# TensorE adds the gathered rows of a graph layer, with chunks paired by kind, slots of 12 passes and edge records of 4

## The reference

```
msg = x[src] + edge_feat
agg = segment_sum(msg, dst, num_segments=12500)
h = relu(agg @ W1 + b1)            # 64 -> 128
out = layernorm(x + h @ W2 + b2)   # 128 -> 64
```

## Time and profile before

| | us |
|---|---|
| median of 3 runs | 1507.69 (1505.83 to 1508.44) |
| the profiled execution, its own time | 1504.08 |
| its span, first to last instruction | 1502.3 |

### The profile page before, as it was taken

How to read it: one execution, slowest core, us unless ns; L and a number is a source line. 1 busy time by engine, 2 the same in 40 slices (tenths; PEclk the granted TensorE clock), 3 DMA queues, 4 the chain that set the end, 5 groups by cost and what they waited for, 6 DMA issues and landing times.

```text
span 1502.3 us, 43214 instructions
## 1 busy us (share of the span) xinstructions
PE 1212.9 (81%) x15541; PEld 979.2 (65%) x15542; DVE 1346.7 (90%) x3537; ACT 840.6 (56%) x1767; POOL 1076.9 (72%) x1139
## 2 busy tenths in 40 slices
PE   1235767778787887888888888899999999999895
PEld 1134656655666776776655555688888888888853
DVE  4659999999999899899999999999999999999644
ACT  1044444668435566567444444567777777766454
POOL 9758777777777777777777777777777777777312
PEclk8555578999999999999999999999999999999997
DMA  2833444444444444444444443444444444433133
GB/s 103 212 85 79 120 113 111 116 111 109 108 115 112 114 115 106 108 109 116 112 114 107 104 117 102 113 112 111 112 112 109 111 113 113 113 100 94 23 79 93
DMA packets 159272, 162.50 MB, mean 108 GB/s; under 512 B 53817, under 2 KB 141801, under 8 KB 158729
## 3 DMA queue, kind: packets, MB, share of 16 engines
q1 hardware_dynamic: 124679, 122.86, 27.9%
q0 software_dynamic: 34384, 36.90, 12.8%
HBM read 154.78 MB, written 4.85 MB: 106 GB/s over the span
## 4 chain that ended last, share of the span: by engine, by line
PE 31%; DVE 29%; issue 16%; POOL 11%; DVEq 4%; ACT 2%; DMA 1%; POOLq 0%; ACTq 0%
PE sums_ps L1092 12%; PE counted_ps L1076 11%; POOL xmsg L572 11%; DVE oh_key L878 10%; DVE oh_lo L874 6%; PE chunk_ps L1059 5%; DVE onehot L835 5%; DVE lists L856 3%; DVE gmsg L828 2%; DVEq L848 2%; PE turn_ps L1104 2%; ACT counts L674 1%; DVE less_b L788 1%; DVEq L856 1%; PE counted_ps L1160 1%
## 5 line engine op out<-in xcount | busy, mean ns | idle before, releaser
L572 POOL DMA_INDIRECT xmsg<-in_x,idx_t x1025 | 995.5, 971 | 322.4 <-issue 307.8
L674 ACT CAST counts<-counted_ps 128x392 bf16<-128x392 f32 (+2 forms) x1375 | 675.2, 545 | 480.6 <-PE counted_ps L1076 468.1
L1076 PE MATMUL counted_ps<-oh_key,oh_lo 128*128 128x196 bf16 (+3 forms) x4206 | 524.7, 255 | 123.2 <-DVE oh_key L878 105.9
L878 DVE TENSOR_TENSOR oh_key<-counted_ps,tables 128x980 bf16<-128x980 f16 (+4 forms) x883 | 541.3, 613 | 0.0
L1092 PE MATMUL sums_ps<-x_parts,counts 128*128 128x193 bf16 (+4 forms) x4410 | 495.0, 249 | 0.3
L1076 PEld LDWEIGHTS counted_ps<-oh_key,oh_lo 128*128 128x128 bf16 x4206 | 290.5, 102 | 227.3 <-DVE oh_key L878 167.0
L1092 PEld LDWEIGHTS sums_ps<-x_parts,counts 128*128 128x128 bf16 (+4 forms) x4410 | 396.3, 109 | 38.6 <-issue 1.9
L874 DVE TENSOR_TENSOR oh_lo<-counted_ps,tables 128x640 bf16<-128x640 f16 (+3 forms) x883 | 412.3, 467 | 9.9 <-PE counted_ps L1076 1.0
L1059 PE MATMUL chunk_ps<-onehot,cmsg 128*64 128x32 f32 (+1 forms) x4200 | 254.1, 231 | 26.2 <-DVE gmsg L828 23.6
L1059 PEld LDWEIGHTS chunk_ps<-onehot,cmsg 128*64 128x64 f32 x4200 | 220.1, 145 | 60.9 <-issue 43.2
L835 DVE TENSOR_TENSOR onehot<-counted_ps,rel_t 128x160 f32<-128x160 f32 (+1 forms) x625 | 234.3, 375 | 0.2
(11 more groups left out here) (96 smaller groups left out, 450.2 us busy)
## 6 DMA issues: line engine op xcount, KB each, us to landing
cmsg<-in_edge_attr SPq DMA_DIRECT2D x420, 160.0 KB
gmsg<-in_edge_attr SPq DMA_DIRECT2D x205, 160.0 KB
xmsg<-in_x,idx_t POOLq DMA_INDIRECT x1025
x_parts<-in_x SPq DMA_DIRECT2D x12, 256.0 KB, 3.4
out_nodes<-x_parts SPq DMA_DIRECT2D x12, 256.0 KB, 2.6
edge_records<-counts SPq DMA_DIRECT2D x1, 1575.0 KB
lists<-in_src SPq DMA_DIRECT2D x1, 1562.5 KB
lists<-in_dst SPq DMA_DIRECT2D x1, 1562.5 KB
```

What stands on the lines that cost most here:

```text
L572: pool.indirect_dma_start(xmsg[:, at * D:(at + 1) * D], None, x, bass.IndirectOffsetOnAxis(ap=idx_t[:, of:of + 1], axis=0)).then_inc(gathe ...
L674: nc.scalar.copy(to, ps.rearrange("p (n h) -> p h n", h=HI)).then_inc(unit_kept, 1)
L878: nc.vector.tensor_tensor(oh_key[s % RING][:, 0:n * w].rearrange("p (k n o) -> p k n o", k=n, o=2), key_ps[:, 0:w].rearrange("p (n o) -> p ...
L1076: mm = nc.tensor.matmul(unit_ps[u % BANKS][:, col:col + slot.key_cols], oh_lo[s % RING][:, n * P:(n + 1) * P], oh_key[s % RING][:, n * slo ...
```

## The change

- `mix` is gone. For a gathered chunk TensorE multiplies the edge rows and then the gathered rows by the same mark, 10 matmuls a chunk instead of 5. `xmsg` has 6 slots instead of 5, freed by TensorE's products instead of by `mix`; `gmsg` has 6 instead of 8.
- Both chunks of a pair are of one kind, and one `mark` instruction makes the mark of both (313 instead of 625). `onehot` has 2 buffers of a pair instead of 4 of a chunk.
- Slots hold up to 12 nodes' worth of passes, and `plan` weighs widths by `85 + 86 * w` instead of `195 + 92 * w`.
- `FINE` is 4 instead of 16, so groups of edges begin at multiples of 4; a row of records is shorter, and 128 edges are still fetched at once. A pass of the search now has a stretch of its own (`Range`: first, step, length): row p of a group is loaded from `first + p * step`. An added small instruction (`begins`, from `row_at`) puts the row's offset to the result. Guard values stand at both ends of `fine_most`.
- `CROWS` is 86 instead of 84: 430 counted chunks and 195 gathered ones.
- Loads and stores with 125 or 86 rows are issued as two DMAs, one of them with a multiple of 16 rows (`in_sixteens`).
- The planned times in `timeline` change, and `TURN_TABLE` and `SUBTRACT` swap their slots.

By the arithmetic of `plan` and `timeline`, with N = 12500 and E = 400000:

| | before | after |
|---|---|---|
| counted nodes | 5716 | 5988 |
| passes of width 1, 2, 3, 4 | 1547, 2006, 75, 578 | 2666, 1545, 335, 0 |
| units of 5, 4, 3 nodes | 241, 1109, 25 | 411, 732, 335 |
| slots, groups, blocks | 883, 33, 45 | 581, 36, 48 |
| indirect gathers | 1025 | 975 |
| searched elements, all groups | 22842 | 29938 |
| slots of width 3 | 26 (of 3 or fewer passes) | 85, the last ones, nearly all of 4 passes and 4 units |

```diff
-            cost = sum(t * (195 + 92 * w) for t in ts) / nodes
+            cost = sum(t * (85 + 86 * w) for t in ts) / nodes
...
-        while (at + n < len(passes) and (at + n) % P and passes[at + n][2] == width and n < 10
-               and (n + 1) * width * hi <= 10 * hi):
+        while (at + n < len(passes) and (at + n) % P and passes[at + n][2] == width and n < SLOT
+               and (n + 1) * width <= SLOT):
...
+        for step in range(counted // FINE // P):
+            first = min(a - p * step for p, a in enumerate(low))
+            length = max(a - p * step for p, a in enumerate(high)) - first
+            if best is None or length < best.length:
+                best = Range(first, step, length)
...
-    cost = [x.n * (195 + 92 * x.width) + 500 for x in slots]
+    cost = [x.n * (67 + 51 * x.width) + 290 for x in slots]
...
-    FIRST, LAST = 90.0, 36.0 + 6.6 * gathered + 1.4 * groups
+    FIRST, LAST = 90.0, 36.0 + 6.45 * gathered + 1.4 * groups
...
+    pairs = [(36.0 + chunk * (k + 2) + 5.0, "gather", k) for k in range(0, gathered - 1, 2)]
+    pairs += [(70.0 + (LAST - 70.0) * (i + 1.) / counted, "count", i) for i in range(0, counted - 1, 2)]
+    pairs.sort()
...
-    GSLOTS, XSLOTS, CSLOTS = 8, 5, 6
+    GSLOTS, XSLOTS, CSLOTS = 6, 6, 6
...
+            for to, of, done in ((src_i, src_v, src_in), (dst_i, dst_v, dst_in)):
+                for a, b in in_sixteens(ROWS):
+                    sp.dma_start(to[a:b, :], of[a:b, :]).then_inc(done, 16)
...
+                sp.dma_start(most_b[g % 2][:, 0:x.length],
+                             bass.AP(most_dram.tensor, FRONT + x.first, [[x.step, P], [1, x.length]])).then_inc(most_in[g % 2], 16)
...
-                    pool.wait_ge(mixed, k - XSLOTS + 1)
+                    pool.wait_ge(summed, PLACE["gather", k - XSLOTS] + 1)
...
+                nc.vector.scalar_tensor_tensor(out=begins[g % 2][:, :], in0=row_at[:, :], scalar=float(x.step),
+                                               in1=run_t[:, g:g + 1], op0=ALU.mult, op1=ALU.add).then_inc(slanted, 1)
...
-            def mark(place, kind, i):
-                c = i if kind == "count" else CCH + i
-                if place >= OSLOTS:
-                    dve.wait_ge(summed, place - OSLOTS + 1)
-                w = width_of(kind, i)
+            def mark(pair):
+                (place, kind, i), n = pair[0], len(pair) * TILES
+                c, w = i if kind == "count" else CCH + i, width_of(kind, i)
+                if place >= 2 * OSLOTS:
+                    dve.wait_ge(summed, place - 2 * OSLOTS + 2)
...
-                pe.wait_ge(mixed, i + 1)
-                return gmsg[:, s * TILES * D:(s + 1) * TILES * D]
+                s, t = i % GSLOTS, i % XSLOTS
+                pe.wait_ge(gin[s], 16 * (i // GSLOTS + 1))
+                pe.wait_ge(gathered[t], 16 * TILES * (i // XSLOTS + 1))
+                return [gmsg[:, s * TILES * D:(s + 1) * TILES * D], xmsg[:, t * TILES * D:(t + 1) * TILES * D]]
```

More of the change, by code:

```diff
@@ L12 @@
 TOP = 256
-CROWS = 84
-FINE = 16
+CROWS = 86
+SLOT = 12
+FINE = 4
 RARE = 1e-7
@@ L19 @@
 Piece = namedtuple("Piece", "unit at cols opens closes")
+Range = namedtuple("Range", "first step length")
 def rare_above(mean, cap):
@@ L128, in timeline @@
         gathers_at[s].append(divmod(g, 5))
-    jobs = [(36.0 + chunk * (k + 1) + 5.0, "gather", k) for k in range(gathered)]
-    jobs += [(70.0 + (LAST - 70.0) * (i + .5) / counted, "count", i) for i in range(counted)]
-    jobs.sort()
+    pairs = [(36.0 + chunk * (k + 2) + 5.0, "gather", k) for k in range(0, gathered - 1, 2)]
+    pairs += [(70.0 + (LAST - 70.0) * (i + 1.) / counted, "count", i) for i in range(0, counted - 1, 2)]
+    pairs.sort()
     jobs_at = [[] for _ in range(S + 1)]
     s = 0
-    for place, (_, kind, i) in enumerate(jobs):
-        t = jobs[min(place | 1, len(jobs) - 1)][0]
+    for q, (t, kind, i) in enumerate(pairs):
         while s < S and begin[s] < t:
             s += 1
-        jobs_at[s].append((place, kind, i))
+        jobs_at[s] += [(2 * q, kind, i), (2 * q + 1, kind, i + 1)]
+    kind, i = ("gather", gathered - 1) if gathered % 2 else ("count", counted - 1)
+    jobs_at[S].append((2 * len(pairs), kind, i))
     return gathers_at, jobs_at
@@ L164, in build @@
     NARROW_ROWS = narrow_chunks(N, E, CHUNK, SLIM, CCH) // TILES
-    width_of = lambda kind, i: SLIM if kind == "count" and i < NARROW_ROWS * TILES else WIN
+    width_of = lambda kind, i: SLIM if kind == "count" and (i | 1) < NARROW_ROWS * TILES else WIN
     HI = -(-N // P)
@@ L265, in build @@
         xmsg = sb("xmsg", [P, XSLOTS * TILES * D])
[L266 to L268 removed]
+        onehot = [sb(f"onehot{s}", [P, 2 * TILES * WIN]) for s in range(OSLOTS)]
+        oh_lo = [sb(f"oh_lo{k}", [P, SLOT * P], bf16) for k in range(RING)]
+        oh_key = [sb(f"oh_key{k}", [P, SLOT * HI], bf16) for k in range(RING)]
         tables = [sb(f"tables{k}", [P, 2 * P, 2], f16) for k in range(TABLES)]
@@ L279, in build @@
         run_t = sb("run_t", [P, GROUPS])
+        row_at = sb("row_at", [P, 1])
+        begins = [sb(f"begins{k}", [P, 1]) for k in range(2)]
         sums = sb("sums", [P, XC])
@@ L889, in _ @@
             for s in range(NS + 1):
-                for place, kind, i in JOBS_AT[s]:
-                    mark(place, kind, i)
-                    if kind == "gather":
-                        mix(i)
-                    if place >= LAG:
-                        add(place - LAG)
+                for k in range(0, len(JOBS_AT[s]), 2):
+                    pair = JOBS_AT[s][k:k + 2]
+                    mark(pair)
+                    for place, _, _ in pair:
+                        if place >= LAG:
+                            add(place - LAG)
                 if s == NS:
```

124 lines of the change are left out of this document (66 added, 58 removed).

## The result

The changed kernel takes 1660.23 us, median of 3 runs (1657.62 to 1665.8), against 1507.69: a ratio of 1.102, interval 1.097 to 1.107. Slower was forecast, but by 11 us, and it is 152. The profiled execution took 1657.62 us, its span is 1655.8.

The account below looks back on a forecast made before the run. GpSimd was taken to set the pace at 1.280 us an instruction. Slot 496 at 1201 plus 223 put the last slot at 1424, 11 later; span 1513, median 1519 us; range 1463 to 1540, the forecast's own 1498 to 1538.

Parts of the forecast that it names:

- What bounds the kernel now: Whole loop: GpSimd sets the pace at 1.280 us an instruction, just ahead of TensorE and VectorE.
- GpSimd's restart: Loop start: first wait, for TensorE's first pair, ends at 89.6 instead of 87.0; GpSimd then ends at 1343, 64 us earlier.
- VectorE, −250 us, free: VectorE's busy time: about 250 us less out of 1347, worth nothing by itself.
- no loss up to slot 496: Loop before width 3: TensorE needs 1.88 us a slot, GpSimd 1.94; slot 496 at 1201.
- The last 85 slots: Width-3 stretch: ScalarE's copies and waits for banks take 223 us, last slot at 1424 instead of 1413.
- waits for banks: Last stretch: three banks hold units, so ScalarE idles while TensorE opens a fourth; 36 us on top of 187.
- rival 1: Last stretch: ScalarE bounds but bank waits stay hidden; stretch 187, last slot 1388, median 1483; chance 0.20.
- Rival 2: Last stretch: copy time goes by elements, 0.39 us a unit; TensorE last with 165, median 1461; chance 0.16.
- runs which cross a 16-byte border pay: ScalarE's 3-node copies: runs of three 2-byte elements cross 16-byte lines in 2 of 8 rows, fitting the long copies.
- Rival 3: Loop start: half clock lasts twice as long, another 35 us lost, 1554; chance 0.06.
- The loop's close: Behind the last slot: loop's close and tail as before, no added time.
- the sign: Whole kernel: slower, 1519 us, last slot 11 us later; chance of slower 0.53, faster 0.39, the same 0.08.

Follow-up runs that it names:

- g7: Changed kernel with at most 3 units a slot, the add two pairs later (LAG 4 for 2) and no width-3 windows: 1448.32 us, 0.962 of the kernel before.
- i8: Changed kernel with at most 3 units a slot, LAG 4, no width 3, and VectorE adding the gathered rows again: 1441.15 us, 0.957 of the kernel before.
- e6: Changed kernel with at most 3 units a slot and the add two pairs later (LAG 4 for 2): 1487.53 us, 0.987 of the kernel before.
- e1: Changed kernel with slots limited to passes of at most 3 units (609 slots for 581): 1542.49 us, 1.023 of the kernel before.
- e2: Changed kernel with VectorE adding a pair's result two pairs later instead of one (LAG 4 for 2): 1589.72 us, 1.054 of the kernel before.

## Why the prediction failed, step by step

**What bounds the kernel now: right.** It rests on GpSimd's 1.280 us an instruction, and g7, where little else hinders GpSimd, has its last gather at 1337.0 (forecast 1343 for its end). That is nearer than it should be: GpSimd restarted there at 94.7 instead of 89.6 and then needed 1.269 us an instruction.

**GpSimd's restart: late by 4.6 us.** In the timeline after it restarts at 94.17 instead of 89.6. The wait itself is 9.16 us (before 10.35); what moved is the start of the loop:

```profile
39.88 1.68 SPq L474 DMA_DIRECT2D onehot<-counts  x2
...
94.17 0.94 POOL L605 DMA_INDIRECT xmsg<-in_x,idx_t  x1 [9.16 <-PE chunk_ps L1092]
```

SyncE's list DMAs start at 39.88 instead of 36.30, since GpSimd writes longer lists, in 38.1 us instead of 34.7. The forecast held up to 2 us possible for the guards, the halves and "768 more list elements" together and put it in the range; it is 3.6, and they stand on the path. The other part of that step was right: VectorE's wait for `src` falls from 17.3 to 10.3 us (its first instruction then takes 7.8 us instead of 3.9, so 3.1 us are left of the 7), and nothing comes of it, since the search then waits for the group's edges queued behind the lists, 17.1 us instead of 13.1, and begins 4.5 later:

```profile
62.27 1.20 DVE L821 TENSOR_SCALAR_CACHE_REDUCE less_b<-most_b,node_t 128x948 bf16<-128x948 int16 x1 [17.08 <-DMA most_b<-fine_most]
```

**VectorE, −250 us, free: size off, reading right.** Busy 1188 instead of near 1100; 159 less. It brought nothing, and in i8 73 us more of it cost nothing.

**TensorE, "no loss up to slot 496": this is the step that failed,** with 125 of the 143 us. Its terms were good. The gathered pair was put at 1.39 us and took 1.32 in the middle (from 4.48 to 5.80 in e6, the rows above: 1004.48 to 1005.80). The need of a slot was put at 1.88 us; e6 goes from slot 258, at 732.1 us, to slot 496, at 1188.7, in 1.92 us a slot, with TensorE busy 97.7% in the stretch shown above, which makes 1.88. What was wrong is what was made of them. A sum of an engine's work set against GpSimd's pace, 1.88 of 1.94, holds only if the engine is never stopped by order. At 97% there is next to no slack, and each wait that stands in the middle of a slot comes on top. The prediction knew the very rule that counted, "TensorE opens the fourth unit of a slot when the first has been kept", and used it for the last 85 slots alone, as if the slots of width 2 touched three units. Six passes of width 2 are 12 nodes, three units of 4 only when a slot begins at a unit's border; 208 of these slots don't. And it had no term at all for `add`'s wait for the products (17.6 us in all before, 260.8 after): it counted 0.47 of a pair a slot, but as work, and didn't ask how far apart the pairs stand when 581 slots hold what 883 held.

The prices by experiment: banks 118 us (e1), lockstep 70 (e2), both 173 (e6). The mark at slot 496: 1326.1 after, 1233.6 in e1, 1269.6 in e2, 1188.7 in e6.

**The last 85 slots: 237 for 223, near, but in part by luck.** ScalarE's copies of 3 nodes have a mean of 682 ns over 335 (642 was taken from 25), those of 5 nodes 708, of 4 nodes 505:

```profile
L707 ACT CAST counts<-counted_ps 128x392 bf16<-128x392 f32 x732 | 311.3, 505 | 271.8 <-PE counted_ps L1108 269.3 <-issue 2.3
...
L707 ACT CAST counts<-counted_ps 128x490 bf16<-128x490 f32 x411 | 260.9, 708 | 267.2 <-PE counted_ps L1108 261.1 <-issue 5.6
L707 ACT CAST counts<-counted_ps 128x294 bf16<-128x294 f32 x335 | 174.8, 682 | 49.6 <-PE counted_ps L1108 48.4
```

Back to back 16 of them took 8.01 us, (8.01 − 0.68) / 15 = 0.49 apart, under the 0.542 of the sum. ScalarE was busy 177 of the 237 us, 75% and not over 80. The case that the sum describes, waits for banks without the lockstep, is e2: 227 us. The case of rival 1, no fourth unit, is e6: 206, its last slot at 1394.8 (forecast 1388), ScalarE busy 84%. In both, as after the change, 8.6 us are a block's multiplies that no step had (see the loop's close); without them they make 218 for 223 and 198 for 187. So the waits for banks cost 21 us and not 36, everything else 11 more than ScalarE's bare need, and the two errors nearly cancel. The other 10 of the 237 came with the lockstep. Rival 1's mechanism was real and became visible once slots touched three units.

**Rival 2, the copy by elements, is refuted for these copies.** A copy of 294 elements takes 35% longer than one of 392, over 335 and 732 of them. The figure of the Trainium skill, "PSUM — Partial Sum Buffer", section "Specifications (TRN2)", 0.83 ns an element, is given there for 2-byte elements written into PSUM; these copies write SBUF. Carried over to them it would make 294 elements 81 ns shorter than 392, and the measurement decides.

That runs which cross a 16-byte border pay, as the prediction offered, can be seen in the trace after, but it is the smaller part. The copies come in the order of the plan's units, whose first row says where in a 16-byte line the runs of 2-byte elements begin, all 98 of a copy alike. Means in ns, with counts:

| run of | elements | no crossing | crossing |
|---|---|---|---|
| 3 | 294 | 636 (255) | 831 (80) |
| 4 | 392 | 502 (727) | 1058 (5) |
| 5 | 490 | 604 (214) | 821 (197) |

A crossing costs about 200 ns in a copy of 98 runs. But runs of 3 that don't cross still take 134 ns longer than runs of 4: of the 177 ns between the two means, crossings explain some 45. Why the rest, no run here shows.

**Rival 3, the low clock:** the first slices stand at 7, 5, 6, 6, 7 against 8, 5, 5, 5, 5 before; no loss to see. (The fives before end at 188 us, five slices of 37.6, not at about 150 as the rival has it.)

**The loop's close: 8.6 us that no step had.** The rows above tell why: two blocks' 98 multiplies each, 8.57 and 8.55 us, stand at the end. The last block has only 36 rows, so it is complete a few slots after the one before it, and neither finds slots over which to be spread. Before, only the last block's stood so (8.60 us, behind the last slot at 1412.8). Now the first of the two stands ahead of the last slot, so its time is in the 237 us, and the tail starts 15.6 us after the last slot, as before (14.6). It is the same in e6 (8.57 and 8.55 us); in g7 both stand behind the last slot.

**As a whole** the sign was right and the size wrong, 1519 for 1660. The sign didn't hang on the failed step (1201 and the 237 us of the last stretch make 1438, still later than the 1413 of before), but most of the loss came from where none was forecast. The range, up to 1540, held every bound of the costs that had been listed, but none for the sum's own assumption that 97% of an engine's time can be used. (Half of 36 either way makes a stretch of 205 to 241 and not 203 to 242; nothing hangs on it.)

## What to carry to other kernels

Where an engine needs 97% of the pace, its sum of work is no forecast; walk one slot of each shape through the order written in the program, and ask at each instruction which buffer it opens and when the one in it was closed. A ring of three banks carries a slot that touches three units and no more: a change of slot size or tiling has to be set against the ring, border by border, over the whole run and not only where the stage looks tight. A lag counted in items of work is only as long as the items stand apart: when the same pairs were spread over a third fewer slots, a lag of one pair, which had cost little, became dear: one constant was worth 70 us.

## What the runs showed of the hardware

- A ScalarE copy from `counted_ps` to bf16 in short runs isn't priced by its elements alone but by how its writes lie: within a 16-byte line, 502 ns for 392 elements in runs of 4, 636 for 294 in runs of 3, 604 for 490 in runs of 5; where the runs cross a 16-byte border, 831 for runs of 3 and 821 for runs of 5.
- With the load of `src` (125 rows of 3200 int32) split into 112 and 13 rows, VectorE waited 10.3 us for it instead of 17.3, and its first instruction was done 3.1 us earlier (at 18.25 us instead of 21.33).
- GpSimd wrote its lists, 8448 elements before and 9216 after, in 34.7 and 38.1 us: 4.1 ns an element, on one partition.
- Chips differ: on some, stretches of TensorE's instructions came some 0.7 us apart, and the same program took 2527 to 2556 us instead of 1507, at a mean granted clock of 0.74 for 0.92. An order tuned on one isn't tuned on the other; there the add on TensorE was no loss.
